# Expert tiles of one and two blocks in a mixture-of-experts stage on one Trainium2 core

## The reference

```python
logits = xf @ Wr.T                                  # 2048 rows, 8 experts
scores, expert = jax.lax.top_k(logits, 2)
weights = jax.nn.softmax(scores, axis=-1)
for e in range(8):
    h = jax.nn.silu(xf @ Win[e].T)                  # 256 -> 512
    y = y + gate[:, e:e + 1] * (h @ Wout[e].T)      # 512 -> 256
x = x + jnp.tanh(g_ffn[1]) * y
```

## Time and profile before

| what | value |
|---|---|
| time, median of 3 runs | 1393.06 us (1390.16 to 1395.96) |
| span of the profiled execution | 1390.6 us |
| the profiled execution's own time | not given apart; the runs shown are those above |
| mean granted TensorE clock | 0.969 |
| PE, PEld, DVE, ACT, POOL busy | 93%, 67%, 76%, 67%, 53% |
| instructions | 30539 |
| the experts' stage, first transposes to read-back | 1229.8 to 1370.1 us |

### The profile page before, as it was taken

One profiled execution on the slowest core, in us unless ns is written; L12 is line 12 of the kernel. 1 busy time (PEld: TensorE's weight loads), 2 busy tenths in 40 slices (PEclk: granted clock), 3 DMA queues, 4 the chain that ended last, 5 costly groups with the idle time before them and its releaser, 6 DMA issues. The chain is left out here.

```text
span 1390.6 us, 30539 instructions
## 1 busy us (share of the span) xinstructions
PE 1286.4 (93%) x8885; PEld 938.2 (67%) x8885; DVE 1054.3 (76%) x2477; ACT 925.3 (67%) x3621; POOL 743.8 (53%) x1099
## 2 busy tenths in 40 slices
PE   3899999999996999999999999999899999669992
PEld 2234444544345888888888888888787878559992
DVE  6456666666676888888888889888788888746664
ACT  1245555454567899899988998899788878323331
POOL 2354646464646556655665566556455788313331
PEclk9799999999998999999999999999999999879996
DMA  5442323233212202202220122112221101522325
GB/s 136 114 76 56 72 55 68 60 59 70 47 51 65 80 2 81 81 13 67 80 80 23 57 80 80 31 48 80 81 81 54 40 32 36 232 88 78 93 82 184
DMA packets 145819, 100.49 MB, mean 72 GB/s; under 512 B 68541, under 2 KB 139198, under 8 KB 145728
## 3 DMA queue, kind: packets, MB, share of 16 engines
q1 hardware_dynamic: 134592, 87.28, 23.5%
q0 software_dynamic: 3744, 8.45, 1.7%
q10 hardware_dynamic: 7392, 3.64, 0.9%
HBM read 58.42 MB, written 42.48 MB: 73 GB/s over the span
## 5 line engine op out<-in xcount | busy, mean ns | idle before, releaser
L1430 POOL TENSOR_TENSOR head_rstd<-head_rstd,minus_half 128x4 f32<-128x4 f32 x192 | 224.8, 1171 | 15.1
L1418 ACT ACTIVATE squares<-ps 128x128 bf16<-128x128 f32 x768 | 201.8, 284 | 46.3 <-PE ps L1381 36.5
L1381 PE MATMUL ps<-w_proj_in,xq 128*128 128x512 f16 (+1 forms) x1024 | 210.1, 328 | 7.0 <-ACT headsT L1454 6.4
L1510 POOL TENSOR_TENSOR prob<-prob,rinv 128x512 f32<-128x512 f32 x128 | 138.4, 1081 | 107.7 <-DVE rinv L1505 107.4
L1497 ACT ACTIVATE prob<-ps,nmax 128x128 f32<-128x128 f32 x512 | 182.2, 390 | 10.3 <-DVE nmax L1488 9.0
L1454 ACT ACTIVATE headsT<-ps,l_hln 128x256 f32<-128x256 f32 (+1 forms) x256 | 167.8, 688 | 31.7 <-PE ps L1445 31.7
L1418 ACT ACTIVATION_READ_ACCUMULATOR squares<-ps 128x1 f32 x768 | 165.2, 216 | 0.0
L1438 DVE TENSOR_TENSOR heads_n<-ps,head_rstd 128x512 f32<-128x512 f32 x192 | 131.3, 684 | 25.0 <-POOL head_rstd L1430 24.8
L728 DVE TENSOR_REDUCE nmax<-ps 128x4 f32<-128x512 f32 x128 | 85.1, 683 | 73.2 <-PE ps L721 73.0
L1481 PE MATMUL ps<-headsT 128*128 128x128 f32 x1024 | 136.5, 276 | 1.0 <-DVE probT L1526 0.4
L1381 PEld LDWEIGHTS ps<-w_proj_in,xq 128*128 (+1 forms) x1024 | 100.5, 98 | 53.9 <-issue 8.2
(11 more groups left out here) (304 smaller groups left out, 2797.3 us busy)
## 6 DMA issues: line engine op xcount, KB each, us to landing
slots<-blank_slot SPq DMA_DIRECT2D x12, 1554.0 KB, 8.8
halves<-half_made SPq DMA_DIRECT2D x32, 256.0 KB, 2.6
w_proj_in<-halves SPq DMA_DIRECT2D x16, 512.0 KB
taken<-slots SPq DMA_DIRECT2D x23, 259.0 KB, 2.8
w_out_raw<-in_wprojT SPq DMA_DIRECT2D x8, 512.0 KB, 3.8
half_raw<-in_winT SPq DMA_DIRECT2D x16, 256.0 KB, 3.0
half_raw<-in_woutT SPq DMA_DIRECT2D x16, 256.0 KB, 3.1
q_stack<-q_parts SPq DMA_DIRECT2D x48, 64.0 KB
```

The costliest lines, as they stand in the source:

```text
L1381: last = e.matmul(out, xq[:, k, which, slot_at], weights(k, hl, c0, n), start=(k == 0 and hl == 0), stop=(k == KD - 1 and hl == 1))
L1418: last = e.activation(squares[:, 4 * n + h, :], A[n][:, h * HD1:(h + 1) * HD1], ACT.Square, scale=HD1**-0.5, accum_out=hss[:, 4 * n + h:4 ...
L1430: e.tensor_tensor(hr[:, four], hr[:, four], t["half"][:, four], ALU.pow).then_inc(g_r[n].sem, 1)
L1510: e.tensor_tensor(prob[:, kind, :, :], prob[:, kind, :, :], spread(rinv[:, kind, :], P), ALU.mult).then_inc(g_p[kind].sem, 1)
```

## The change

The tiles are no longer all of one size. `SIZES` holds 15 tiles of two blocks of 128 rows and behind them 9 of one, 39 blocks in all, which is 2 x 16 + 8 - 1. The table now counts blocks of 128 rows. It gives each expert its pairs of blocks first, expert after expert (`wide`), and the odd block that remains, where there is one, a place at the end (`odd`). A tile's place is `nth`, in blocks: 0, 2, ... 28, then 30, 31, ... 38. Where there are more than 15 pairs, the others are taken as two tiles of one block. The comparison array has 17 columns in place of 9 (`ge` in bf16, `rise` beside it), 408 elements of a partition, and the chain has 17 links.

In a tile of one block, SyncE loads 128 packets, `turn` has 4 transposes, `lift` copies 512 elements, `hidden` has 24 matmuls with 128 moving rows, whose result fills one PSUM bank, `silu` and `parts` handle one piece of 512, `down` has 12 matmuls, and there is one scaling and one scatter. `aim` has the same six instructions, on one element of a partition. The semaphores' counts go by `DONE`, the running sum of the sizes. The order of the queues and the ring of 3 stay.

```diff
-    c_choose, c_place, c_table = Chain(nc, "c_choose", 14), Chain(nc, "c_place", 3), Chain(nc, "c_table", 11)
+    c_choose, c_place, c_table = Chain(nc, "c_choose", 14), Chain(nc, "c_place", 3), Chain(nc, "c_table", 17)
...
-        e.memset(reach[:, NE:NE + 1], float(NE * SHELF - 2 * B * P))
-        e.iota(nth_i[:, :], pattern=[[1, WORDS * WORD]], base=0, channel_multiplier=0).then_inc(makes, 1)
+        e.memset(reach[:, NE:NE + 1], float(P * (NE * SHELF // P - (2 * B - NE))))
+        e.memset(owned[:, 0:NE], 1.0)
+        e.memset(owned[:, NE:NE + 1], 0.0)
+        e.memset(owned[:, NE + 1:NE + 2], float(1 - NE))
+        e.memset(owned[:, NE + 2:2 * NE + 1], 1.0)
+        e.iota(nth_i[:, 0:WIDE], pattern=[[2, WIDE]], base=0, channel_multiplier=0)
+        e.iota(nth_i[:, WIDE:WORDS * WORD], pattern=[[1, WORDS * WORD - WIDE]], base=2 * WIDE,
+               channel_multiplier=0).then_inc(makes, 1)
...
-        chain.link(e.tensor_scalar(tiles[:, :], S[1][:, 0:NE], 1.0 / TR, (TR - 1.0) / (2 * TR), ALU.mult, ALU.add))
-        chain.link(e.tensor_scalar(tiles[:, :], tiles[:, :], MAGIC, MAGIC, ALU.add, ALU.subtract))
-        chain.link(e.tensor_tensor(prior[:, :, :], upto[:, :, :], tiled(tiles[:, :], NE + 1), ALU.mult))
-        chain.link(e.tensor_reduce(start[:, :], prior[:, :, :], AX, ALU.add))
-        e.scalar_tensor_tensor(reach[:, 0:NE], start[:, 0:NE], -float(TR), shelf[:, :], ALU.mult, ALU.add)
-        chain.link(e.tensor_tensor(ge[:, :, :], spread(nth[:, :], NE + 1), tiled(start[:, :], WORDS * WORD), ALU.is_ge))
-        chain.link(e.tensor_reduce(owner[:, :], ge[:, :, 0:NE], AX, ALU.add))
-        chain.link(e.tensor_tensor(ge[:, :, :], ge[:, :, :], tiled(reach[:, :], WORDS * WORD), ALU.mult))
-        chain.link(e.tensor_reduce(spot[:, :], ge[:, :, :], AX, ALU.max))
-        chain.link(e.scalar_tensor_tensor(spot[:, :], nth[:, :], float(TR), spot[:, :], ALU.mult, ALU.add))
+        wide, odd, last = runs[:, 0, :], runs[:, 1, :], 2 * NE + 1
+        prior = rise[:, :, :].rearrange("p u n -> p (u n)")[:, 0:2 * (NE + 1) * NE]
+        prior = prior.rearrange("p (w m n) -> p w m n", w=2, m=NE + 1)
+        chain.link(e.tensor_scalar(blocks[:, :], S[1][:, 0:NE], 1.0 / P, (P - 1.0) / (2 * P), ALU.mult, ALU.add))
+        chain.link(e.tensor_scalar(blocks[:, :], blocks[:, :], MAGIC, MAGIC, ALU.add, ALU.subtract))
+        chain.link(e.tensor_scalar(wide, blocks[:, :], 0.5, -0.25, ALU.mult, ALU.add))
+        chain.link(e.tensor_scalar(wide, wide, MAGIC, MAGIC, ALU.add, ALU.subtract))
+        chain.link(e.scalar_tensor_tensor(odd, wide, -2.0, blocks[:, :], ALU.mult, ALU.add))
+        chain.link(e.tensor_tensor(prior, upto[:, :, :].unsqueeze(1).to_broadcast([P, 2, NE + 1, NE]),
+                                   runs[:, :, :].unsqueeze(2).to_broadcast([P, 2, NE + 1, NE]), ALU.mult))
+        chain.link(e.tensor_reduce(before_run[:, :, :], prior, AX, ALU.add))
+        e.tensor_scalar(start[:, 0:NE + 1], before_run[:, 0, :], 2.0, None, ALU.mult)
+        e.tensor_scalar(spot[:, 0:1], before_run[:, 1, NE:NE + 1], -1.0, float(BLOCKS), ALU.mult, ALU.add)
+        chain.link(e.scalar_tensor_tensor(spot[:, NE:2 * NE], wide, 2.0 * P, shelf[:, :], ALU.mult, ALU.add))
+        chain.link(e.tensor_scalar(start[:, NE + 1:last], before_run[:, 1, 0:NE], spot[:, 0:1], None, ALU.add))
+        e.scalar_tensor_tensor(reach[:, 0:NE], start[:, 0:NE], -float(P), shelf[:, :], ALU.mult, ALU.add)
+        chain.link(e.scalar_tensor_tensor(reach[:, NE + 1:last], start[:, NE + 1:last], -float(P), spot[:, NE:2 * NE],
+                                          ALU.mult, ALU.add))
+        e.tensor_copy(step[:, 0:1], reach[:, 0:1])
+        e.tensor_tensor(step[:, 1:last], reach[:, 1:last], reach[:, 0:last - 1], ALU.subtract)
+        chain.link(e.tensor_tensor(ge[:, :, :], spread(nth[:, :], last), tiled(start[:, :], WORDS * WORD), ALU.is_ge))
+        chain.link(e.tensor_tensor(rise[:, :, :], ge[:, :, :], tiled(step[:, :], WORDS * WORD), ALU.mult))
+        chain.link(e.tensor_tensor(ge[:, :, :], ge[:, :, :], tiled(owned[:, :], WORDS * WORD), ALU.mult))
+        e.tensor_reduce(spot[:, :], rise[:, :, :], AX, ALU.add)
+        chain.link(e.tensor_reduce(owner[:, :], ge[:, :, :], AX, ALU.add))
+        chain.link(e.scalar_tensor_tensor(spot[:, :], nth[:, :], float(P), spot[:, :], ALU.mult, ALU.add))
         e.tensor_copy(shelf_row[:, :], spot[0:1, :])
         chain.link(e.scalar_tensor_tensor(eights[0:1, :], owner[0:1, :], -1.0, eights[0:1, :], ALU.add, ALU.mult))
         e.tensor_scalar(owner[:, :], owner[:, :], -1.0, float(NE + 1), ALU.mult, ALU.add)
 }
 
 
+BLOCKS = 2 * B + NE - 1
+WIDE = 15
+SIZES = (2,) * WIDE + (1,) * (BLOCKS - 2 * WIDE)
+DONE = tuple(itertools.accumulate(SIZES, initial=0))
 TS = 2
-TR = TS * P
-TILES = 2 * B // TS + NE - 1
...
+    def puts(n):
+        return 16 * sum(SIZES[n % RING:n:RING])
+
     @block.sync
     def _(e):
         e.wait_ge(t["tabled"], 1)
...
             if n >= RING:
                 e.wait_ge(s_turn, n - RING + 1)
                 e.wait_ge(s_part, n - RING + 1)
-            row = e.value_load(shelf_row[0:1, n:n + 1], min_val=0, max_val=SLOTS - TR)
-            e.dma_start(taken[:, n % RING, :, :],
-                        slots[bass.ds(row, TR), :].rearrange("(s p) w -> p s w", p=P)).then_inc(got[n % RING], 16)
+            row = e.value_load(shelf_row[0:1, n:n + 1], min_val=0, max_val=SLOTS - size * P)
+            e.dma_start(taken[:, n % RING, 0:size, :],
+                        slots[bass.ds(row, size * P), :].rearrange("(s p) w -> p s w", p=P)).then_inc(got[n % RING], 16)
 
     @block.tensor
...
         def turn(n):
+            size = SIZES[n]
             e.wait_ge(got[n % RING], 16 * (n // RING + 1))
             if n >= 2:
                 e.wait_ge(s_xT, n - 1)
             for c in range(2 * KD):
-                for h in range(TS):
-                    last = e.transpose(turned[n % 2][:, c * TR + h * P:c * TR + (h + 1) * P],
+                for h in range(size):
+                    last = e.transpose(turned[n % 2][:, (c * size + h) * P:(c * size + h + 1) * P],
                                        taken[:, n % RING, h, :].bitcast(F16)[:, c * P:(c + 1) * P], ident_h[:, :])
             last.then_inc(s_turn, 1)
...
         def hidden(n):
+            size = SIZES[n]
+            rows, each = size * P, KF // size
...
             for m in range(KF):
-                if n >= 2 and m % 2 == 0:
-                    e.wait_ge(s_h, 2 * (n - 2) + m // 2 + 1)
+                if n >= 2 and m % each == 0:
+                    e.wait_ge(s_h, DONE[n - 2] + min(m // each + 1, SIZES[n - 2]))
...
                     for part, hl in ((0, 0), (0, 1), (1, 0)):
                         w = win[:, hl, bass.ds(mine, 1), k, m * P:(m + 1) * P].rearrange("p e n -> p (e n)")
-                        last = e.matmul(Hb[2 * (n % 2) + m // 2][:, m % 2 * TR:(m % 2 + 1) * TR], w,
-                                        xT[:, n % 2, part * KD + k, :],
+                        c = (part * KD + k) * rows
+                        last = e.matmul(Hb[2 * (n % 2) + m // each][:, m % each * rows:(m % each + 1) * rows], w,
+                                        xT[:, n % 2, c:c + rows],
                                         start=(k == 0 and part == hl == 0), stop=(k == KD - 1 and part == 1))
-                if m % 2:
+                if m % each == each - 1:
                     last.then_inc(s_H, 1)
 
         def down(n):
+            size = SIZES[n]
+            each = KF // size
             mine = expert(n)
             if n >= 2:
                 e.wait_ge(s_y, n - 1)
-            for h in range(TS):
+            for h in range(size):
                 for m in range(KF):
-                    if h == 0 and m % 2 == 0:
-                        e.wait_ge(s_hh, 4 * n + 2 * (m // 2) + 2)
+                    if h == 0 and m % each == 0:
+                        e.wait_ge(s_hh, 2 * (DONE[n] + m // each) + 2)
                     for part, hl in ((0, 0), (0, 1), (1, 0)):
                         w = wout[:, hl, bass.ds(mine, 1), m, :].rearrange("p e n -> p (e n)")
-                        last = e.matmul(Yb[n % 2][:, h * D:(h + 1) * D], hh[:, n % 2, part, m, h * P:(h + 1) * P], w,
+                        c = (m * size + h) * P
+                        last = e.matmul(Yb[n % 2][:, h * D:(h + 1) * D], hh[:, n % 2, part, c:c + P], w,
                                         start=(m == 0 and part == hl == 0), stop=(m == KF - 1 and part == 1))
             last.then_inc(s_Y, 1)
 
...
         def lift(n):
+            wide = 2 * KD * SIZES[n] * P
             e.wait_ge(s_turn, n + 1)
             if n >= 2:
-                e.wait_ge(s_H, 2 * (n - 1))
-            e.tensor_copy(xT[:, n % 2, :, :].rearrange("p c t -> p (c t)"), turned[n % 2][:, :]).then_inc(s_xT, 1)
+                e.wait_ge(s_H, DONE[n - 1])
+            e.tensor_copy(xT[:, n % 2, 0:wide], turned[n % 2][:, 0:wide]).then_inc(s_xT, 1)
...
```

(42 more changed lines are left out.)

22 lines of the change are left out of this document (9 added, 13 removed).

## The result

The changed kernel takes 1376.38 us (median of 4 runs, 1374.10 to 1376.90) against 1393.47 (median of 4, 1390.16 to 1395.96) for the one before: a ratio of 0.988, 95% interval 0.986 to 0.990. The forecast was 1376.8. The profiled execution took 1374.1 us, with a span of 1372.3.

The account below looks back on a forecast made before the run. TensorE's work per tile was taken to bound the kernel, in narrow tiles its sequencer's address steps. Stage 12.9 and tail 3.4 saved, together 16.3 us, taken from the median 1393.06, gave 1376.8 us; range 1370 to 1384.5.

Parts of the forecast that it names:

- Wide tiles, 13 x 5.69: Experts stage, hidden 1 to 14: wide tiles keep every instruction and stay 5.69 us apart, 73.9 us in all.
- Two narrow hiddens behind wide downs: Hidden 15 and 16: the sequencer runs ahead behind wide downs, so 2 x (0.22 + 2.62 + 1.34) = 8.4 us.
- The narrow period: Hidden 17 to 23: copy, then TensorE's sequencer giving out hidden's addresses, set 3.45 us per narrow tile, 24.2 in all.
- The array-bound rival: Narrow tiles: the sequencer keeps ahead, period 2.88 us, 4.0 us more saved, 1372.8 us; chance 0.12.
- The latency rival: Narrow tiles: the copy or the ring of three loads is late, period 4.05, 1381.0 us; chance 0.22.
- The ring has no slack left: Tile loads: the round of three buffers takes 10.1 us, 3.4 per narrow tile, level with the sequencer.
- Stage and tail: Experts: stage 106.5 against 119.4 us, 12.9 saved; last hidden to read-back 6.9 against 10.3, 3.4 saved.
- The clock rival: Narrow tiles' holes drop TensorE to 1.2 GHz, a narrow tile takes 5.76 us, 1395.6 us in all; chance 0.04.
- The table: Before the experts: VectorE's longer chain adds about 3.0 us, hidden behind the scatters by 0.6; cost zero, bounds 0 and 1.5.

Follow-up runs that it names:

- the spaced order: The changed kernel's same 24 tiles reordered, narrow ones mostly in pairs between wide ones; 1373.76 us, ratio 0.987 to the kernel before; repeated, 1373.88 us.

## Why the prediction was right, step by step

- **Wide tiles, 13 x 5.69**: as forecast. **Two narrow hiddens behind wide downs**, 4.2 each: 4.18.
- **The narrow period.** 3.45 was forecast, 3.56 measured, 0.8 us over the seven. The mechanism held: steps at 124 ns, one behind the other, and hidden spread over 1.84 to 2.00 us for its 23 spacings in six of the seven (1.62 in the first). Two terms were a little small, and the 16 addresses took 1.98 in place of 2.1. From the last address step to the last matmul are 0.39 us (1333.38 to 1333.77), not 0.25. And the sequencer does not give out down during the transposes and the copy from time zero, but begins 0.12 later, and takes 1.14 from down's first step to hidden's. So 0.39 + 0.12 + 1.14 + 1.98 = 3.63. I had let the copy and the sequencer come out level (0.91 against 1.0). The copy has 0.44 us to spare, and the run with fixed addresses in down shows about that margin by itself.
- **The array-bound rival** (2.88) fell: removing the address steps brings 2.87, and the changed kernel has 3.56. Its price was right, 2.87 is the array's period. The Trainium skill, "TensorE: Matmul & The Clock Gate", section "Back-to-back issue gap", gives about 81 ns for such a stream. The trace agrees in size (80 to 87 ns) where the weights' addresses come from a register, and not where they are fixed or given out ahead (56 ns, 1.28 us for 23 spacings). Taken as a limit of the array, the page would leave fixed addresses and the spaced order without a gain.
- **The latency rival** (4.05, every narrow tile) fell. Its cause exists, but in another form. The 0.6 us of the earlier trace rows is a copy whose signal arrives late, while the silu of the same rows is on time. It comes and goes between executions of one kernel (in no tile of the first profile of the changed kernel, in tiles 6 to 14 of the next). Where it reaches the narrow tiles it is 1.7 to 2.0 us, once, and makes one interval 4.9 in this kernel. That is the 1.3 us between the two profiles of the unaltered kernel.
- **The ring has no slack left**: half right. With four places nothing changes in this kernel. As soon as the sequencer is out of the way, the ring costs 2.4 us of the stage.
- **Stage and tail.** 12.9 and 3.4 forecast, 12.2 and 3.2 measured: 15.4 against 16.3. That the median came within 0.4 us of the forecast is partly luck. The medians of the result's runs differ by 17.1 us, more than the two terms give, and the end of the second hidden moves by 5 us from profile to profile, with the return of the full clock. The forecast had nothing for that.
- **The clock rival** fell. The granted clock is 1.00 (2.4 GHz) from 1236.0 to 1344.8, wide tiles and narrow ones alike.
- **The table.** Its chain took 3.64 us and now takes 6.61 (from the first link at 1217.60 to the end of the word at 1224.21): 3.0 more, as forecast, and it hides. The last write of the table and SyncE's wait for the scatters, by their lines:

```profile
L2045 DVE CAST owner_word<-spot x1: 155/155/155, 1224.1 to 1224.1; 1x3 int32<-1x3 f32 x1
...
L2165 SPq EVENT_SEMAPHORE  x1: 17/17/17, 1225.3 to 1225.3; - x1
```

The cover was 1.1 us, not 0.6, partly for a reason that I had not seen. I took the last four of the routing's scatters as fixed, and they are not. Their line in the kernel after (min/median/max):

```profile
L1988 POOL DMA_INDIRECT slots<-r_packet,r_at_u x4: 971/974/1342, 1218.5 to 1222.7; - x4
```

All four took 0.97 before. Now the third takes 1.34, so the last starts 5.00 us behind the end of `r_at_u` and not 4.63. These scatters are on the path, so the longer table costs 0.37 us that I had put at zero. All 13 profiles with the new table have it, always at the third (1.33 to 1.34). A VectorE operation of 408 elements with two inputs is under way when it starts, in the kernel after:

```profile
1220.95 0.58 DVE L2036 TENSOR_TENSOR rise<-ge,run_step 128x408 f32<-128x408 bf16 x1
1221.04 1.34 POOL L1988 DMA_INDIRECT slots<-r_packet,r_at_u  x1 [0.30 <-issue]
```

That operation ends 0.49 us behind the scatter's start, and the scatter takes 0.37 more than 0.97. The Trainium skill, "SBUF — State Buffer", section "SBUF: two separate sides", says that a VectorE operation with two inputs in SBUF and a GpSimd operation that reads SBUF shut one another out of a shared port, for the whole of the one that came first. The traces agree, by all 82 scatters of the 14 profiles behind 1215 us that start while such a TENSOR_TENSOR is under way. Where it ends 0.14 to 0.65 us behind the scatter's start, the scatter is longer by that time less 0.12 to 0.13 (55 scatters). Where it ends sooner, nothing is added (15). Where it had begun 0.02 to 0.04 before the scatter, it is the TENSOR_TENSOR that is longer, 741 to 764 ns in place of 693 (12). Of the 499 scatters that start beside none, the longest took 1.01; a `SCALAR_TENSOR_TENSOR` on one element a partition, under way until 0.22 behind the start, adds nothing, though it has two inputs in SBUF too. The run with the longer table fits. Its five comparisons fill 1220.71 to 1223.75, and two scatters start beside them. The comparison under way ends 0.49 us behind the start of the first, and only 0.08 behind that of the second. The timeline of that run:

```profile
1220.71 3.04 DVE L2036 TENSOR_TENSOR ge<-nth,run_start 128x408 bf16<-128x408 f32 x5
1221.41 1.34 POOL L1988 DMA_INDIRECT slots<-r_packet,r_at_u  x1 [0.30 <-issue]
1223.06 0.97 POOL L1988 DMA_INDIRECT slots<-r_packet,r_at_u  x1 [0.31 <-issue]
```

**What stays open.** What makes TensorE's signals late, whether the scatters have a part in it, and why an execution has it or not. What brings the full clock back sooner in one execution than in another. Fewer address steps per matmul, which would attack the bound itself, were not tried. Nor was another number of wide tiles. An order that ends on a wide tile and a narrow one was, and its tail was 1.9 us longer.

**A faster version.** The spaced order is the best kernel here that computes the whole: 1373.8 us, 2.6 us (0.2%) below the changed kernel, ratio 0.987 to the one before. That is a small gain: the slowest of its runs (1374.94) lies above the fastest of the changed kernel's (1374.10).

## What to carry to other kernels

Halving a tile halves the array's work only. The instructions per tile that the sequencer gives out (address steps, waits) stay, and the period becomes the larger of the two: count both before choosing a tile size. Where both sizes exist, mix them, so that the sequencer runs ahead during a wide piece and uses that up in a narrow one; this took the sequencer's 0.6 us out of every narrow tile, though late signals took some of it back. Start a scatter on GpSimd where VectorE is not in the middle of an operation with two inputs in SBUF: here it cost up to 0.5 us. A busy share of 100% in which the same matmuls take 1.9 us in place of 1.34 is no full engine: compare the length of equal pieces in the chain.

## What the runs showed that I had not expected

- Steps of TensorE's sequencer that work out an address from a register come 124 ns apart. At two steps for three matmuls of 128 columns they set 80 to 87 ns per matmul, against 56 with fixed addresses or with the sequencer ahead.
- TensorE's signal for the copy on VectorE arrived 0.6 us late in some stretches, with ScalarE's on time. Once in seven of eight profiles the signals to both arrived 1.7 to 2.2 us late, beside GpSimd's scatters back to back (1.28 us apart). The one profile without scatters had no late copy, but neither had one with them.
- One of GpSimd's last four scatters of the routing was stretched from 0.97 to 1.34 us by a VectorE operation with two inputs in SBUF that was under way at its start. By 82 such scatters the stretch is the time to the end of that operation less 0.12 us, and nothing where it ends sooner.
